# Cross-attention with eight rounds per batch instead of four per head pair, projections moved between the rounds' products, and the output product split in two parts

## What is computed

```python
q = (x @ w_q).reshape(B, Sq, 16, 64).transpose(0, 2, 1, 3)        # x: 4 x 512 x 256, after a layer norm
k = (context @ w_k).reshape(B, Skv, 16, 64).transpose(0, 2, 1, 3) # context: 4 x 1024 x 192
v = (context @ w_v).reshape(B, Skv, 16, 64).transpose(0, 2, 1, 3)
attn = jax.nn.softmax(jnp.einsum('bhid,bhjd->bhij', q, k) * 64 ** -0.5, axis=-1)
out = jnp.einsum('bhij,bhjd->bhid', attn, v)
return out.transpose(0, 2, 1, 3).reshape(B, Sq, 1024) @ w_o + b_o
```

## Time and profile before

| stage | us in the profile |
|---|---|
| norm phase with the context, to the first load of attention | 38.3 |
| attention 0: first load to the first `transpose_max` | 32.9 |
| attention 0: first to last `transpose_max` (31 segments) | 891.2 |
| attention 0: last segment to its end | 31.2 |
| layer 0 experts with norm and router, and the norm behind | 633.8 |
| attention 1, from its first load | 960 |
| rest | 264 |
| span | 2851.0 |
| this execution's own time | 2852.76 |

### The profile page before, as it was taken

One profiled execution on the slowest core, in us unless ns is written; L12 is line 12 of the kernel. 1 busy time (PEld: TensorE's weight loads), 2 busy tenths in 40 slices (PEclk: granted clock), 3 DMA queues, 4 the chain that ended last, 5 costly groups with the idle time before them and its releaser, 6 DMA issues. The chain is left out here.

```text
span 2851.0 us, 40294 instructions
## 1 busy us (share of the span) xinstructions
PE 2647.2 (93%) x13254; PEld 1814.1 (64%) x13254; DVE 1999.4 (70%) x2552; ACT 1290.9 (45%) x1891; POOL 1336.2 (47%) x1054
## 2 busy tenths in 40 slices
PE   3999999999999879999999689999999999996895
PEld 2556565656565468888888555656565656554785
DVE  5677677777676567777777657677777767764795
ACT  3545454545454333333333344545454545443394
POOL 4665656565656501111111145656666565652245
PEclk9999999999999989999999789999999999997997
DMA  3111111111111020000000010111111101103312
GB/s 109 39 30 33 30 29 33 37 26 35 35 24 33 16 67 22 24 26 22 22 28 17 10 39 23 41 29 33 29 36 27 40 22 38 27 23 116 121 50 86
DMA packets 48850, 108.85 MB, mean 38 GB/s; under 512 B 7200, under 2 KB 22432, under 8 KB 47776
## 3 DMA queue, kind: packets, MB, share of 16 engines
q1 hardware_dynamic: 43952, 101.01, 12.5%
q0 software_dynamic: 1536, 4.20, 0.5%
q10 hardware_dynamic: 3312, 3.02, 0.3%
HBM read 47.64 MB, written 10.22 MB: 20 GB/s over the span
## 5 line engine op out<-in xcount | busy, mean ns | idle before, releaser
L372 POOL TENSOR_TENSOR L1a_psums<-L1a_psums,L1a_probs 128x512 f32<-128x512 f32 x384 | 481.3, 1302 | 50.0 <-ACT L1a_probs L407 50.0
L372 POOL TENSOR_TENSOR L0a_psums<-L0a_psums,L0a_probs 128x512 f32<-128x512 f32 x384 | 481.1, 1297 | 49.7 <-ACT L0a_probs L407 49.7
L471 DVE TENSOR_REDUCE L1a_row_max<-psum 128x2 f32<-128x2048 f32 x128 | 293.5, 2293 | 150.9 <-PE psum L584 150.8
L471 DVE TENSOR_REDUCE L0a_row_max<-psum 128x2 f32<-128x2048 f32 x128 | 293.5, 2293 | 150.7 <-PE psum L584 150.7
L802 POOL TENSOR_TENSOR L0e_w_lo<-L0e_raw,L0e_w_hi 128x768 fp32r<-128x768 f32 x34 | 63.7, 1873 | 497.7 <-ACT L0e_w_hi L816 497.7
L407 ACT ACTIVATE L1a_probs<-psum 128x1024 f32<-128x1024 f32 x256 | 253.4, 1025 | 76.7 <-PE psum L611 75.2
L407 ACT ACTIVATE L0a_probs<-psum 128x1024 f32<-128x1024 f32 x256 | 253.3, 1025 | 73.8 <-PE psum L611 72.2
L624 PE MATMUL psum<-L0a_probs,L0a_v 128*64 128x512 f32 x1024 | 247.3, 605 | 0.0
L624 PE MATMUL psum<-L1a_probs,L1a_v 128*64 128x512 f32 x1024 | 247.3, 604 | 0.0
L856 DVE SCALAR_TENSOR_TENSOR xres<-psum,L0e_weights_of,xres 128x256 f32<-128x256 f32 x544 | 225.6, 477 | 22.7 <-PE psum L1029 21.8
L372 POOL TENSOR_TENSOR L1a_psums<-L1a_probs 128x512 f32<-128x512 f32 x64 | 81.4, 1294 | 322.1 <-ACT L1a_probs L407 322.1
(11 more groups left out here) (348 smaller groups left out, 6224.4 us busy)
## 6 DMA issues: line engine op xcount, KB each, us to landing
L0a_k_hs<-L0a_k_st SPq DMA_DIRECT2D x64, 256.0 KB, 3.5
L1a_k_hs<-L1a_k_st SPq DMA_DIRECT2D x64, 256.0 KB, 3.4
L0e_raw<-in_experts SPq DMA_DIRECT2D x34, 384.0 KB, 3.0
L1weights<-in_sorted SPq DMA_DIRECT2D x2, 6144.0 KB, 17.9
L0a_q_hh<-L0a_q_hh SPq DMA_DIRECT2D x64, 128.0 KB, 2.3
L1a_q_hh<-L1a_q_hh SPq DMA_DIRECT2D x64, 128.0 KB, 2.3
L0a_raw<-in_attention SPq DMA_DIRECT2D x8, 384.0 KB, 3.2
L1a_raw<-in_attention SPq DMA_DIRECT2D x8, 384.0 KB, 3.1
```

The lines of the kernel that those rows point to most:

```text
L372: nc.gpsimd.tensor_tensor(psums[:, h, :], a, probs[:, h, kv, :], ALU.add).then_inc(sem["acc"], 1)
L471: nc.vector.reduce_max(row_max[:, qt, 0:2 * 32].rearrange("p (h n) -> p h n", h=2)[:, :, 0], psum[:, 0:4 * BANK].rearrange("p (h k) -> p h ...
```

## The change

Batches are now the outer loop and head pairs the inner one, and all 32 segments are written out, with constants in every wait. Segment i is head pair i % 8 of batch i // 8.

- **Context.** Only one batch's context is loaded and split ahead of the attention; the three arrays hold two batches. The next batch's is loaded, rounded on ScalarE and subtracted on GpSimd in segments 0, 1 of each batch (`prepares`).
- **Weights.** Key, query and output weights come in one load of 128 x 768 per segment (35 a layer), value weights in one of 128 x 512 per two segments; ScalarE makes the hi part, GpSimd the lo part.
- **Values** are projected for two head pairs at once: 256 columns per matmul, five matmuls per 128 keys, two pieces of 256 keys per segment, behind `qk` 2 and `qk` 4. ScalarE copies the finished piece of 128 x 512; VectorE no longer adds.
- **Queries** of i + 1 stand behind `transpose_max`; VectorE makes both their parts.
- **Keys** of i + 2 are projected in halves, in turns 0 and 1 of the second part.
- **Turns**: `score` stands first and two `pv` behind it. `total` stands at the segment's end, ahead of the next `transpose_max`.
- **Output**: `o_sb` is split (ScalarE hi, VectorE lo), and each half is six fp32r matmuls of 256 columns instead of two fp32 ones; the halves stand around `qk` 7.
- The bias is added on VectorE in four instructions ahead of segment 0, not on GpSimd in 16.

TensorE in `L0a_`, from the third query/score turn of a segment to the next: this is the place where `score` waits for VectorE's maximum and where K was taken in. Names: `L0a_k_st,L0a_q_hh` is a `score`, `L0a_probs,L0a_v` are two `pv`, `ctx_*,L0a_w_split` of 512 columns are keys, and of 256 and 128 are values.

Behind `qk` 7 stood two `pv`, and the first `score` behind them; now half of the output product stands there and the `score`, which waits for the last exponential. The diff, cut to its core:

```diff
-                            for n in range(NCH):
-                                src = ctx_top if n < BATCH else ctx_bot
-                                sp.dma_start(stage[:, n, :], src[:, chunk(n)]).then_inc(sem[f"staged{n}"], 16)
+                            for n, src in enumerate((ctx_top, ctx_bot)):
+                                sp.dma_start(stage[:, n, :], src[:, 0:SKV]).then_inc(sem[f"staged{n}"], 16)
...
+                    PLACE = dict(MT=2, Q=6, K0=6, K1=5, TOTAL=7, OUT0=7, OUT1=5, VA=5, VB=4)
...
+                        def segment(i):
+                            n = prepares(i)
...
+                            if i % 2 == 0 and i // 2 + 2 < PAIRS:
+                                load_values(i // 2 + 2)
+                            if i + 4 < WEIGHTS:
+                                load_weights(i + 4)
+                            if i + 1 < SEGMENTS:
+                                copy_queries(i + 1)
+                            if i + 2 < SEGMENTS:
+                                copy_keys(i + 2)
...
+                        def low_weights(n):
+                            pool.wait_ge(sem["whi"], n + 1)
+                            nc.gpsimd.tensor_tensor(w_split[:, n % 2, 1, :], raw[:, :], w_split[:, n % 2, 0, :], ALU.subtract)\
+                                .then_inc(sem["wlo"], 1)
...
+                            max_rows(i)
+                            for p in range(3):
+                                exps(i, p)
+                            if i > 0:
+                                high_output(i - 1)
+                            exps(i, 3)
+                            if pair < PAIRS:
+                                values(pair, n)
+                            exps(i, 4)
+                            exps(i, 5)
+                            if pair < PAIRS:
+                                values(pair, n + 1)
+                            exps(i, 6)
+                            exps(i, 7)
...
+                        def segment(i):
+                            if i + 1 < SEGMENTS:
+                                low_keys(i + 1, 1)
+                            if i > 0:
+                                normalise(i - 1)
+                                low_output(i - 1)
+                            if i + 1 < SEGMENTS:
+                                high_queries(i + 1)
+                                low_queries(i + 1)
+                            if i > 0:
+                                add_output(i - 1)
+                            if i + 1 < SEGMENTS:
                                 for qt in range(QT):
+                                    maximum(i + 1, qt)
+                                    if qt == 1 and i + 2 < SEGMENTS:
+                                        low_keys(i + 2, 0)
...
+                            dst = bank(PLACE["VA" if n % 2 == 0 else "VB"])
+                            for t in range(2):
+                                cols = slice((2 * n + t) * P, (2 * n + t + 1) * P)
+                                hi, lo, hl = (c[:, b % 2, cols] for c in (ctx_hi, ctx_lo, ctx_hl))
+                                last = split_product(dst[:, t * 2 * P:(t + 1) * 2 * P],
+                                                     [(hi, wv[:, 0, WV[0]]), (hi, wv[:, 1, WV[0]]), (lo, wv[:, 0, WV[0]]),
+                                                      (hl, wv[:, 0, WV[1]]), (hl, wv[:, 1, WV[1]])])
...
+                            for t in range(2):
+                                rows = slice((2 * half + t) * P, (2 * half + t + 1) * P)
+                                last = split_product(bank(PLACE[f"OUT{half}"])[:, t * DIM:(t + 1) * DIM],
+                                                     [(o_hi[:, rows], w_hi), (o_hi[:, rows], w_lo), (o_lo[:, rows], w_hi)])
...
+                        def segment(i):
+                            pair, n = i // 2 + 1, i % 2 * 2
+                            transpose_max(i)
+                            if i + 1 < SEGMENTS:
+                                queries(i + 1)
+                            for p in range(3):
+                                qk(i, p)
+                            if pair < PAIRS:
+                                project_values(pair, n)
+                            qk(i, 3)
+                            qk(i, 4)
+                            if pair < PAIRS:
+                                project_values(pair, n + 1)
+                            qk(i, 5)
+                            qk(i, 6)
+                            if i > 0:
+                                output(i - 1, 0)
+                            qk(i, 7)
+                            if i > 0:
+                                output(i - 1, 1)
+                            FILL = ((0, 1), (2, 3), (4, 5), (6, 7))
                             for qt in range(QT):
+                                if i + 1 < SEGMENTS:
+                                    score(i + 1, qt)
+                                for kv in FILL[qt]:
+                                    pv(i, kv)
+                                if qt < 2 and i + 2 < SEGMENTS:
+                                    keys(i + 2, qt)
+                            total(i)
```

More of the change, by code:

```diff
@@ L183, in _ @@
                                 .then_inc(sem["hi"], 1)
[L184 to L185 removed]
+                            if source is not None and g < NCH:
+                                context(g)
                     @block.tensor
@@ L309, in half_of, with prepares @@
+                    def half_of(n):
                         return slice(n * BANK, (n + 1) * BANK)
-                    def run(eng, segment):
-                        segment(0, 0, first=True)
-                        with eng.Fori(0, HP - 1) as hp:
-                            for b in range(1, BATCH + 1):
-                                segment(hp, b)
-                        for b in range(1, BATCH):
-                            segment(HP - 1, b, ahead=b < BATCH - 1)
+                    def prepares(i):
+                        return i // HP * 2 + i % HP if i % HP < 2 and (i // HP < BATCH - 1 or again) else None
@@ L682, in _ @@
-                        pe.wait_ge(sem["one"], 5)
-                        keys("K0", 0, 0, first=True)
-                        keys("K1", 0, 0, first=True)
-                        queries(0, 0)
-                        for piece in VALUES:
-                            project_values(piece, 0, 0, added=False)
-                        for qt in range(QT):
-                            score(0, 0, qt, first=True)
-                        run(pe, segment)
-                        total(HP - 1, BATCH - 1, ahead=False)
+                                pe.wait_ge(sem["olo"], i + 1)
@@ L692, in _ @@
+                        pe.wait_ge(sem["one"], 5)
+                        for i in range(SEGMENTS):
+                            segment(i)
                         for half in range(2):
-                            output(HP - 1, BATCH - 1, half, ahead=False, last_one=True)
+                            output(SEGMENTS - 1, half)
         expert_sems = sems(stack, "e", "rt pad ready rhi rlo logits copied turned scores step bias const picked counted taken placed "
@@ L1291, in build @@
         norm_phase("n_", xres, x_tiles)
-        attention_phase("L0a_", w["attention"], w["out"], w["out_bias"], xres)
+        attention_phase("L0a_", w["attention"], w["values"], w["out_bias"], xres, again=True)
         norm_phase("L0n_", xres, wipe=sorted_x, clear=attention_sems.values())
@@ L1297, in build @@
         norm_phase("L1i_", xres, clear=expert_sems.values())
-        attention_phase("L1a_", w["attention"], w["out"], w["out_bias"], xres)
+        attention_phase("L1a_", w["attention"], w["values"], w["out_bias"], xres, again=False)
         ctx_scope.close()
```

611 lines of the change are left out of this document (307 added, 304 removed).

## The result

The changed kernel takes 2835.98 us (median of 4 runs, 2835.13 to 2838.42), the one before in the same comparison 2854.86 (4 runs, 2852.27 to 2859.61). The ratio is 0.9933, with a 95% interval of 0.9916 to 0.9951: 14 to 24 us faster. The forecast was 2865 us, with a range that began at 2838 and a chance of 0.25 for faster.

What follows compares the result with a forecast made beforehand. TensorE's own row of work was taken as the bound: 27.52 us work plus 1.47 waits gave 28.99 a segment against 28.74, +14.5 together; with the phase's ends +9.5, put at +8: median 2865 us, range 2838 to 2885.

Steps and rivals of the forecast that it cites:

- all three waits: TensorE waits per segment: before `qk` 2 0.44 us, `score` of turn 0 0.53, `score` of turn 3 0.50; sum 1.47.
- The norm phase: Phase of 38.3 us preparing two context chunks instead of eight, with less VectorE interference: -8 us together.
- segment 30: Segment left with neither values nor K; waits take back half: -2.5 us a layer, -5 in all.
- the tail: End of the phase: output split in series, less a shorter product; +0.8 us a layer, +1.6 in all.
- the stretch ahead of segment 0: Before segment 0: weights split twice in series and more TensorE work, partly at lower clock; +2 us a layer, +4.
- the pricing of the work on TensorE: Sum of matmul groups in one segment's new order: 27.52 us, 0.8 less than before without its wait.
- K's two halves: Two K halves per segment, each behind fp32 `pv`: 5 x 0.235 us plus 0.14 for the switch, 2.62 together.
- the rival of more switches: `score` and `pv` entries on TensorE cost 0.19 us for leaving fp32: some +0.3 a segment, +17, 2882 us; chance 0.2.
- the chain from `qk` 7: `qk` 7 start to `score` of turn 0, through the last exponential: 1.10 + 1.03 + some 0.05 = 2.18 us.
- the exposed switches are not there: Rival: weights load ahead while `pv` runs on TensorE; some -0.45 us a segment, -26, 2839 us; chance 0.27.
- Half of 0.14 for each of two halves of K: Allowance that K's switch costs half as much: -0.02 of the 0.25 us a segment, -1.5 in all.
- Segment 0: Bias between last maximum and low K makes values wait: +1.2 us a layer, +2.4 in all.

## Why the prediction was wrong

- **Terms that held.** Twelve small matmuls at 0.119 each, `qk` at 0.94, `score` at 0.66, the output's 1.42 without a switch behind it. The places of all three waits, that `total` waits for nobody, and that GpSimd, SyncE and the low K are covered. The norm phase (-7.2 for -8), segment 30 (-3.1 for -2.5 each), the tail (+1.6 for +1.6), the stretch ahead of segment 0 (+2.6 for +4).
- **The step that failed** is the pricing of the work on TensorE, 27.52 for 26.90. `transpose_max` was taken at 0.59, a distance that had been read in front of `total`; the change puts it in front of Q, where it is 0.41 (and Q 0.06 less). `pv` was given 0.10 at each of four entries, because the change from values to `pv` seemed to cost that; an entry from `score` costs nothing, -0.40. The last `pv` now stands in front of `total`, at 1.77, -0.10. Against that K's two halves took 0.10 more than forecast: the entry cost 0.10 and not 0.14 each, but the `score` behind each half came 0.09 later, which the sum had not priced; the rival of more switches had it, at just that size. With +0.02 each for `score` and `total` and -0.01 each for values and output, together -0.62.
- **The waits** were 0.22 longer than forecast (0.66 for 0.53 and 0.59 for 0.50), for two reasons. For `score` 3, work that is shorter waits longer for the same chain: turn 2 went from 2.63 to 2.54 in front of a chain of 3.13, which was right. For `score` 0 the chain from `qk` 7 is 225.88 - 223.57 = 2.31, not 2.18. It was built from single durations; the earlier trace rows had a distance of the same kind, 2.32, and it was the better guide.
- **Sum.** -0.62 + 0.22 = -0.40 a segment, 58 times, is -23 of the 23.9 us that were off.
- **The rival that came closest** was the one that said the exposed switches are not there: -0.45 a segment and 2839 us, against -0.40 and 2836. Its figure was right, in part by luck, and its mechanism only in part. The entries of `pv` are free, as it said; K's is not (0.34 to the second matmul, as the forecast wrote, also behind `score`), and 0.28 of the gain came from neighbours that it did not mention. The trace of before shows `transpose_max` in front of `total` only; the 0.59 should have been an upper end, since the edit changed what follows, and not a value.
- **Two slips in the sums.** Half of 0.14 for each of two halves of K is 0.14 less a segment, some 8 us, and not 0.02 and 1.5; the median would then have been about 2858. And four `pv` entries at 0.19 instead of 0.10 are 0.36, not 0.20, so the rival of more switches should have lain higher. Neither changes the sign.
- **Segment 0.** +1.2 a layer was forecast for the bias, by the right mechanism: values wait for the low K behind it. At full clock that wait would be some 2.4 us, an estimate. It was not seen, since the granted clock of 0.51 held TensorE's row to the same point. The result was +2.0 in attention 0, where the clock had been full before, and nothing in attention 1, where it had been low. The forecast had counted the lower clock only ahead of segment 0.
- **The page.** For 256 columns TensorE: Matmul & The Clock Gate ("Back-to-back issue gap") of the Trainium skill gives 262 cycles, an estimated 0.109 us at 2.4 GHz, by which the 20 value matmuls would take 2.18 us. They took 2.37, as the earlier trace rows said.

## What to carry to other kernels

Price a group of matmuls by its distance to the next start with the same neighbours, and when an edit changes a neighbour, treat the price as open on both sides. A group costs something once, so count the groups and not the operations. Where the waits are chains of known length (2.3 from one `qk` to the next but one, 3.13 from `score` to `score`), lay the free work so that each chain has a filler: here the new orders, with fewer groups and a shorter segment 0, took 121 us more off, six times what the change itself did. And when one limit is lifted and nothing is won, look for a second that ends at the same time: here the clock and the bias held segment 0 to the same 0.2 us.

## What was not expected of the hardware

- Two `pv` take 1.87, one 1.01, three 2.73: 0.86 each and 0.15 once, of which 0.10 goes when `total`, with tiles of the same form, follows (1.77).
- A group in front of one with another form of tile ends 0.09 later: K in front of `score` or `pv`, the output in front of `pv` or `score`. The first K matmul behind either takes 0.34 instead of 0.235.
- Matmuls that compute nothing of use can cost almost twice their length: behind an idle time of 3.2 us, at a clock that had already fallen, twelve took 5.04 us instead of 2.8. Begun in that idle time itself (eleven and nine, which left 0.50 and 0.19 idle), they kept the granted clock at 1.00 up to segment 0.
- A wait of 3.13 us in a full row (values behind the bias) was followed by matmuls at the lower level, 1.2 GHz, while waits of 0.66 and less in every segment left the clock at full.
